# Beginning the transposing transfers of the token groups on ScalarE's queue instead of SyncE's, one piece later

## The reference, cut to what matters

```
x = x + 0.5 * ffn(layernorm(x));  x = x + attn(layernorm(x));  x = x + 0.5 * ffn(layernorm(x))

ffn(x):                                   # "thought" is one vector per batch
    thought = layer_norm(x)[:, -1, :] @ agg_w + agg_b
    4 times: thought += gelu(layer_norm(thought) @ d1_w + d1_b) @ d2_w + d2_b
    return layer_norm(x + sigmoid(x @ gate_w + gate_b) * (thought @ bc_w + bc_b))
attn(x):                                  # windows of 128 tokens, each with the one before it
    q, k, v = split(x @ w_attn.T);  s = masked(q @ k.T / 128);  return (relu(s)**2 @ v) @ w_o.T
```

## Time and profile before

| what | us |
|---|---|
| median of 3 runs | 1985.16 (1983.47 to 1986.96) |
| the profiled execution, its own time | 1987.91 |
| its span in the trace | 1986.7 |
| PE busy | 1941.8 (98%) |
| DVE busy | 1300.3 (65%) |
| ACT busy | 662.1 (33%) |
| DMA, mean busy share of the queue's 16 engines | 80.1% |

### The profile page before, as it was taken

The page is one execution under the profiler, slowest core; times in us unless marked ns, Lnnn a source line. Parts: engine busy times, 40 slices in busy tenths (PEclk is TensorE's granted clock), DMA queues, the critical chain, the costliest instruction groups (busy, mean ns, idle before and its releaser), DMA issues.

```text
span 1986.7 us, 30999 instructions
## 1 busy us (share of the span) xinstructions
PE 1941.8 (98%) x12136; PEld 1034.7 (52%) x12136; DVE 1300.3 (65%) x2318; ACT 662.1 (33%) x961; POOL 169.1 (9%) x278
## 2 busy tenths in 40 slices
PE   8999999999999999999999999999999999999997
PEld 3334444444444466666655666556666564444443
DVE  2656785324544666678778656766657638888887
ACT  1555464213332322232334211222112224444442
POOL 0000010000100100111000000000000001111111
PEclk9999999999999999999999999999999999999999
DMA  9899987899999653489989899998899965555552
GB/s 367 340 345 367 390 330 289 304 358 363 356 388 408 231 171 107 153 276 339 314 262 342 263 375 314 312 316 303 290 358 302 320 231 176 146 153 152 156 149 74
DMA packets 275217, 555.81 MB, mean 280 GB/s; under 512 B 149040, under 2 KB 149248, under 8 KB 274688
## 3 DMA queue, kind: packets, MB, share of 16 engines
q1 hardware_dynamic: 275072, 553.83, 80.1%
HBM read 406.93 MB, written 113.26 MB: 262 GB/s over the span
## 4 chain that ended last, share of the span: by engine, by line
PE 37%; DMA 5%; DVE 5%; SPq 2%; issue 1%; ACT 1%; POOL 0%; DVEq 0%; ACTq 0%
PE product_banks L1130 33%; PE product_banks L1264 2%; DMA thought_units<-parts_scratch 2%; PE thought_acc L1329 2%; DMA gate_arena<-arena 1%; DMA arena<-gate_scratch 1%; SPq L1051 1%; DVE bn_parts L1561 1%; DMA thought_units<-in_d_w 1%; SPq L913 1%; DMA arena<-in_x 0%; DVE thought_units L1967 0%; DVE arena L1742 0%; DVE arena L1737 0%; DVE arena L1728 0%
## 5 line engine op out<-in xcount | busy, mean ns | idle before, releaser
L1130 PE MATMUL product_banks<-gate_arena,arena 128*128 128x512 f16 x1536 | 346.4, 379 | 0.0
L1130 PE MATMUL product_banks<-wide_a,thought_units 128*128 128x512 f16 x1536 | 331.7, 379 | 0.0
L1130 PE MATMUL product_banks<-gate_arena,wide_a 128*128 128x256 f16 x2688 | 306.7, 275 | 8.8 <-DMA gate_arena<-arena 8.8
L1130 PE MATMUL product_banks<-wide_b,gate_arena 128*128 128x512 f16 x1344 | 299.2, 379 | 0.0
L1130 PEld LDWEIGHTS product_banks<-gate_arena,wide_a 128*128 128x128 f16 x2688 | 263.3, 99 | 56.3 <-issue 22.5
L1130 PEld LDWEIGHTS product_banks<-gate_arena,arena 128*128 128x128 f16 x1536 | 147.6, 98 | 189.2 <-issue 28.6
L1130 PEld LDWEIGHTS product_banks<-wide_a,thought_units 128*128 128x128 f16 x1536 | 150.3, 98 | 181.2
L1130 PEld LDWEIGHTS product_banks<-wide_b,gate_arena 128*128 128x128 f16 x1344 | 129.5, 98 | 157.4 <-issue 11.3
L1561 DVE BATCH_NORM_STATS2 bn_parts<-arena 128x6 f32<-128x512 f32 x256 | 164.2, 683 | 5.9 <-DMA arena<-in_x 1.4
L2031 POOL TENSOR_TENSOR token_stats<-stats,minus_half 128x1 f32<-128x1 f32 x96 | 68.1, 710 | 974.3 <-DVE stats L1569 795.8
L1586 DVE SCALAR_TENSOR_TENSOR arena<-product_banks,inverse_gate,arena 128x512 f32<-128x512 f32 x64 | 47.9, 749 | 122.9 <-PE product_banks L1130 81.6
(11 more groups left out here) (223 smaller groups left out, 2353.1 us busy)
## 6 DMA issues: line engine op xcount, KB each, us to landing
thought_units<-parts_scratch SPq DMA_DIRECT2D x275, 512.0 KB, 7.5
thought_units<-in_d_w SPq DMA_DIRECT2D x174, 512.0 KB, 7.6
arena<-in_x SPq DMA_DIRECT2D x64, 512.0 KB, 9.1
parts_scratch<-thought_units SPq DMA_DIRECT2D x64, 512.0 KB, 6.0
x_scratch<-arena SPq DMA_DIRECT2D x64, 512.0 KB, 9.0
thought_row<-in_d_w SPq DMA_DIRECT2D x50, 512.0 KB, 8.1
arena<-x_scratch SPq DMA_DIRECT2D x40, 512.0 KB, 7.2
gate_scratch<-arena SPq DMA_DIRECT2D x32, 512.0 KB, 8.8
```

Of the source, the lines that this page charges most:

```text
L1130: mm = pe.matmul(bank, left(i, k), right(j, k), start=(n == 0), stop=(n == 3 * KD - 1))
```

## The change

The branch for `group_turn` leaves the program of SP and stands, word for word but for the engine, in the program of ACT. One `("rest",)` more stands ahead of it in `plan_prep`, so that a tile takes 15 entries.

```diff
@@ plan_prep
-                ("prep_stats", u), ("rest",), ("x1_store", u), ("prep_h1", u), ("rest",), ("prep_low", u),
+                ("prep_stats", u), ("rest",), ("x1_store", u), ("prep_h1", u), ("rest",), ("prep_low", u), ("rest",),
                 ("group_turn", u)]
@@ sync_program, taken out
-            elif kind == "group_turn":
-                u, = a
-                n, i = divmod(u, GROUP)
-                sp.wait_ge(lows_made, u + 1)
-                if n >= 4:
-                    sp.wait_ge(product_full, tokens_read(n - 2))
...
-                sp.dma_start_transpose(
-                    group_of(n).rearrange("p h k t -> p (h k) t")[:, :, i * P:(i + 1) * P],
-                    pg_slots[u % PREP_RING].bitcast(F16)).then_inc(group_in[i], 16)
@@ scalar_program, put in behind prep_h1
+            elif kind == "group_turn":
+                u, = a
+                n, i = divmod(u, GROUP)
+                act.wait_ge(lows_made, u + 1)
+                if n >= 4:
+                    act.wait_ge(product_full, tokens_read(n - 2))
...
+                act.dma_start_transpose(
+                    group_of(n).rearrange("p h k t -> p (h k) t")[:, :, i * P:(i + 1) * P],
+                    pg_slots[u % PREP_RING].bitcast(F16)).then_inc(group_in[i], 16)
```

More of the change, by code:

```diff
@@ L1455, in scalar_program @@
                 act.copy(in_parts(pg_slots[u % PREP_RING])[:, 0], hb).then_inc(h1_ready, 1)
+            elif kind == "group_turn":
[4 more added lines that the diff above has]
+                    act.wait_ge(product_full, tokens_read(n - 2))
+                elif n >= 2:
+                    act.wait_ge(product_full, BANK_AT[("gate", TILES - 1, 1)] + 1)
+                    act.wait_ge(gate_saved, 16 * KD)
+                else:
+                    for slot in FOR_SPLITS:
+                        await_left(act, THOUGHTS.first_left[slot])
+                act.dma_start_transpose(
+                    group_of(n).rearrange("p h k t -> p (h k) t")[:, :, i * P:(i + 1) * P],
+                    pg_slots[u % PREP_RING].bitcast(F16)).then_inc(group_in[i], 16)
             elif kind == "q" and a[1] % 2:
```

## The result

The changed kernel took 2124.42 us in the median of 4 runs (2111.85 to 2127.91) against 1984.32 us before: a ratio of 1.0697, 95% interval 1.0675 to 1.072, or 140 us slower. Forecast were 1986 us and a range of 1973 to 2012. The profiled execution of the changed kernel is the fastest of the four (2111.85 us), so its rows account for 124 of the 140 us.

The account below looks back on a forecast made before the run. PE, busy for 1941.8 of 1986.7 us, was taken as the bound. Terms of -1, -3.6 (waits for the transposing transfer), +3.5 and +2 gave +1 us on the 1985.2 median: 1986 us, range 1973 to 2012.

Parts of the forecast that it names:

- The "holding" rival: At the second tile's transfer, ACT is held as long as SP was, 7 us, landing in 9: +30 us, 2015, chance 0.27.
- How long it takes on a queue of its own: Transposing transfer on ACT's queue: fair share of busy engines, 6.6 us to landing, ACT held for 4.6.
- The upper end, 13.38: Upper bound for a transfer's landing on its own queue, taken from a landing on SP in the kernel before: 13.38 us.
- "ACT held": ACT's work behind the transfers, such as the fourth v product's high part, is late but mostly fits: +2 us.
- The two covers named: For ACT's holding: three more q or v banks, 5.5 us each, and PE waiting for the next group anyway.
- "Start: 4.3 us later": The second transfer's start on ACT: 2.2 us for the score, 0.6 for DVE's order, 1.5 for the first transfer's holding.
- a slack of 0 to 3.2 us a boundary: Time to spare at the group boundaries shown before a later landing delays PE; 2 us was taken.
- The terms for SP: Loads behind the 32 issues taken from SP go out up to 8 to 11 us sooner: -1 us.
- The +3.5 us for ten boundaries: Ten group boundaries with slack, where transfers now landing quickly on SP would land later and delay PE: +3.5 us.
- The 12 us estimated in the prediction: Landing of a transfer on ACT's queue if engines alternate queues by packets: nine turns behind a 1.3 us load each.

Follow-up runs that it names:

- e3: The changed kernel, with SP waiting at each transposing transfer's old place until it has landed, so SP issues nothing behind it: 2034.7 us, ratio 1.0253.
- e6: The changed kernel with most split-weight loads of the second block cut to a quarter of their columns: 1995.7 us, against 1966.1 for the kernel before with the same cut.
- e4: The kernel before with the extra rest, transfers on SP, and ACT held some 5 us by 22 tiny copies at the changed kernel's places: 2062.7 us, ratio 1.0397.
- e1: The kernel before with only the extra rest put in, transposing transfers still on SP: 2012.9 us, ratio 1.0145.
- e16: The kernel before with two rests ahead of the second tile's transposing transfer alone, the preparation left in place: 2008.5 us, ratio 1.0125.
- e2: The changed kernel without the extra rest, transposing transfers on ACT: 2103.6 us, ratio 1.0608.
- e17: The kernel before plus three end blocks: transposing transfer on ACT beside 16 SP loads, on SP behind 16, on ACT beside 32; landings 22.0, 15.5, 25.0 us.
- e15: The kernel before plus four end blocks: transposing transfer on SP among loads (landed 9.4 us), on ACT beside 16 (18.2), alone (4.3); plain ACT load beside 16 (4.7).
- e12: The kernel before, transposing transfers on SP, with only the preparation's x loads issued on ACT: 2011.8 us, ratio 1.0147.

## Why the prediction was wrong

**What held.** PE is the bound and a wait of PE costs its clock too: busy time rose by 29.8 us. ACT's holding was put at 4.6 us and measured 5.2 in the median. The x fetch was issued before the second turn landed (1479.95 against 1497), and ACT's wait for it fell, from 163.7 to 122.3 us in all; the idle time at that instruction did not (163.7 and 163.0), since other waits took its place. The "holding" rival named the right place (between the scores' high parts and the v product's) and the right sign, with 0.27.

**The step that failed first** is "How long it takes on a queue of its own": "of the 4.3 us ... the other 2.3 double. That is 6.6 to landing." It took a fair share of busy engines, in which small and large packets cost the turn alike. The runs show a share by packets, and the turn has 2080 of them, nearly all of 256 B: in the blocks by themselves 18 to 25 us beside full-size loads, and in the changed kernel 14.7 to 27.3 in the four late turns shown. "It is nearer to the lower end because the loads issued before it are no longer in front" had the reason the wrong way round: in one queue, later loads stand behind the turn, and on two they don't. SP, freed from waiting, issued more of them. The upper end, 13.38, came from rows of one queue and bounded nothing. The count of 2330 packets a turn (2080 measured) was in the text, but only for a rival at 0.27, and that rival kept 9 us to landing. e3 puts the worth of this step, with the longer holding that comes with it, at 90 of the 140 us; e6 confirms it from the other side.

**The second** is "ACT held", +2 us. e4 gives 49.8 us for 5 us of holding at both turns. The two covers named, the four banks and PE's idle time before the next group, are not enough: the collects wait for the v product 31.3 us in 11 groups and for the scores 14.4 us in 5. Why the scores too was not tried apart.

**The third** is the moved place, priced within "Start: 4.3 us later" and a slack of 0 to 3.2 us a boundary. On SP alone it costs 28.6 us (e1), 25 of them by the second turn's place in SP's queue (e16). The terms for SP were -1 us; what was missed is that its place also decides which loads, and which stores that have to wait, are in front. The +3.5 us for ten boundaries is the sum of the two that were worked out (1.8 and 1.7); the others, gains and losses, were put at nothing. One of the two, at 1516.04, was also read 0.6 us too early: with no backlog a turn lands 4.3 us after its issue, not 2.0 behind the end of it. PE waited at ten boundaries, not at three.

The parts don't simply add: 28.6 for the rest, 49.8 more for the holding, and the 61.7 that then remain to the changed kernel are the late landing with all that follows it; counted from the other end, e3 gives 90 for the landing and the longer holding together. e2 shows why: without the rest the wait only changes its place.

The statement of the Trainium skill quoted in the prediction ("DMA: Bandwidth & Descriptors", section "Queues, rings and completion order") has the engines go round the queues by packets, which there are groups of descriptors, while the profile counts each piece as a packet. The runs agree that the engines go round and don't share by bytes. The typical 9 to 17 descriptors to a packet that the Trainium skill gives did not hold for these transfers: the start times show one 256 B piece for each 4 KB (e17). The 12 us estimated in the prediction, with a whole load for each packet of the turn, is too low against the 18 to 25 us measured. The same page of the Trainium skill, section "Issuing engines are not separate DMA queues", says that a second issuer saves issue time only; here it cost 140 us, or 119 without the rest (e2).

## What to carry to other kernels

A transfer made of many small pieces belongs in the same queue as the large ones around it, in front of those that are not urgent. On a second queue it takes turns by the packet: here 130 packets an engine beside 4 KB ones took 18 to 25 us to land in place of 4.3, and with most of the loads in 1 KB rows 4.6 in the median. Count its packets, and look at the size of the others'. A queue that is freed from a wait will issue sooner: count what it then puts beside the transfer you meant to speed up. And an issue that can hold an engine for up to 12 us, as here while the neighbour's queue was full, should not stand in a compute engine's order ahead of work that PE needs.

## What was not expected

While the first queue is full, the issuer on the second can be held too: ACT was held for 11.3 us by a turn that had its own queue to itself (e17, third block), but for 2.2 in the first block, at the same distance behind the first load. What decides between the two is open.

In the changed kernel there are stretches in which both queues had work and the engines moved little: 151 GB/s from 1484 to 1489 with their share at 1.25 (the row above). The block of e17 kept some 400 GB/s while the turn's packets went; the second of e15 moved only 269 to 286 from 2016 to 2022. The queues of the changed kernel from 1480 to 1489:

```profile
q10 hardware_dynamic: 946, 0.24, 92.8%
q1 hardware_dynamic: 311, 1.13, 33.8%
```

The turn's own pace is that of e17: 946 packets in 9 us, or a round of sixteen each 0.15 us, against 1058 in 10 us there, and the rounds start 0.17 us apart in both. What is missing is the large packets, three small ones to one in place of one to one. The share says that a small packet holds its engine for 0.14 us in the mean (92.8% of 16 engines and 9 us over 946), against 0.018 in e17 (11.9% of 10 us over 1058). That reads as if all sixteen engines go through the turn in step, at the pace of those that still have large packets; the trace doesn't name a packet's engine, so it isn't shown. It would explain why few large packets are enough to make a turn late (e12). Why so few large ones moved, with the seven transfers that SP had issued since 1478 under way, is left open.
